# Reordering the turns of the local attention's software pipeline in an eight-core transformer kernel

## The reference

```python
q = l2norm(q) * qs;  k = l2norm(k) * ksc
q, k = rotary_xpos(q, k)
bq = q.reshape(b, h, w, 512, d) * 8.0
bk, bv = look_around(k windows), look_around(v windows)   # this window and the one before
sim = jnp.einsum('bhwid,bhwjd->bhwij', bq, bk)
mask = (i < j) | (i > j + 512) | (j == -1)
attn = softmax(where(mask, -max, sim), axis=-1)
out = jnp.einsum('bhwij,bhwjd->bhwid', attn, bv)
x = x + out @ wo
x = x + (a * gelu(g)) @ w2 + b2      # a, g = split(layernorm(shift(x)) @ w1)
```

## Time and profile before

| | us |
|---|---|
| median of the timed runs (2) | 6040.22 (6033.57 to 6046.87) |
| profiled execution, device time | 5998.51 |
| span of its slowest core (core 4) | 5996.8 |
| spans of the eight cores | 5910.4 to 5996.8 |
| PE, matmuls busy | 2880.4 (48%) |
| DVE busy | 2177.7 (36%) |
| ACT busy | 1038.4 (17%) |

### The profile page before, as it was taken

How to read it: one execution, slowest core, us unless ns; L and a number is a source line. 1 busy time by engine, 2 the same in 40 slices (tenths; PEclk the granted TensorE clock), 3 DMA queues, 4 the chain that set the end, 5 groups by cost and what they waited for, 6 DMA issues and landing times.

```text
span 5996.8 us, 43264 instructions; the slowest of 8 cores (5910.4 to 5996.8 us)
## 1 busy us (share of the span) xinstructions
PE 2880.4 (48%) x12576; PEld 1358.3 (23%) x12752; DVE 2177.7 (36%) x4629; ACT 1038.4 (17%) x1989; POOL 38.2 (1%) x46
## 2 busy tenths in 40 slices
PE   3322222232445454543776664454554545678632
PEld 2222222111212212221332221212221222233211
DVE  3666666642323323232233212323232332223324
ACT  0222222210211213031111101303121121011100
POOL 0000000000000000000000000000000000000000
PEclk9666666655556565655887776565555656698865
DMA  5000000014010010104500021010101008000022
GB/s 90 1 0 0 1 0 0 0 63 89 1 42 0 1 42 1 42 1 74 98 8 28 28 47 35 1 42 1 42 1 42 0 1 151 28 29 1 28 70 84
DMA packets 92663, 182.15 MB, mean 30 GB/s; under 512 B 2064, under 2 KB 20752, under 8 KB 92304
## 3 DMA queue, kind: packets, MB, share of 16 engines
q0 software_dynamic: 30176, 61.32, 6.4%
q1 hardware_dynamic: 62256, 118.07, 6.3%
HBM read 177.78 MB, written 54.53 MB: 39 GB/s over the span
## 4 chain that ended last, share of the span: by engine, by line
PE 44%; DVE 32%; issue 8%; DMA 7%; ACT 4%; another core or an unknown queue 3%; DVEq 2%; ACTq 0%; SPq 0%; POOL 0%; POOLq 0%
PE pb_l L1559 6%; PE pa_l L1034 5%; PE pa_l L1303 4%; PE pbf_l L1237 3%; PE bsa_l L1265 3%; DMA YBF<-ysp 3%; DVE RRF L1193 3%; PE pba_l L1509 3%; PE pbg_l L1523 3%; PE pb_l L1523 3%; PE pb_l L1509 3%; DMA ysp<-YBF 2%; PE pa_l L1149 2%; PE pa_l L1163 2%
## 5 line engine op out<-in xcount | busy, mean ns | idle before, releaser
L1237 PE MATMUL pbf_l<-CBF,PRB_l 128*128 128x128 bf16 x1280 | 177.4, 303 | 787.9 <-DVE PRB_l L1228 753.2
L1277 DVE CAST OH_l<-bsa_l 64x128 bf16<-64x128 f32 x256 | 72.4, 283 | 844.9 <-PE bsa_l L1265 844.9
L1559 PE MATMUL pb_l<-HACT_l,W2P_l 128*128 128x512 bf16 x1378 | 333.7, 405 | 44.8 <-DVE YBF L1575 29.4
L1205 ACT ACTIVATE PRB_l<-pa_l,RRF 128x512 bf16<-128x512 f32 x256 | 175.9, 687 | 979.6 <-DVE RRF L1201 975.9
L1237 PEld LDWEIGHTS pbf_l<-CBF,PRB_l 128*128 128x128 bf16 x1280 | 116.9, 131 | 840.1 <-issue 840.1
L634 PE MATMUL pb<-XKk,WR 128*128 128x256 bf16 x512 | 74.9, 321 | 384.1 <-DVE XKk L625 384.1
L1509 PE MATMUL pba_l<-HB_l,W1I_l 128*128 128x512 bf16 x690 | 183.8, 411 | 157.2 <-DVE HB_l L1486 115.9
L1303 PE MATMUL pa_l<-OH_l,WOF_l 64*128 64x512 bf16 x512 | 220.9, 628 | 32.3 <-DVE YBF L1317 27.4
L1009 PE MATMUL pa_l<-WQKV_l,HQ_l 128*128 128x512 bf16 x248 | 70.5, 453 | 311.7 <-DVE YLC L1000 160.7
L1250 ACT ACTIVATE PTB_l<-pbf_l 128x640 bf16<-128x640 bf16 x256 | 180.3, 704 | 206.8 <-PE pbf_l L1237 206.8
L1050 ACT ACTIVATE SQB_l<-pa_l 128x512 bf16<-128x512 f32 x64 | 38.2, 597 | 952.9 <-PE pa_l L1034 948.2
(11 more groups left out here) (223 smaller groups left out, 4460.1 us busy)
## 6 DMA issues: line engine op xcount, KB each, us to landing
YBF<-ysp SPq DMA_DIRECT2D x16, 2048.0 KB, 10.9
ysp<-YBF SPq DMA_DIRECT2D x16, 2048.0 KB, 7.2
W1I_l<-w1i POOLq DMA_DIRECT2D x10, 2048.0 KB, 54.7
W2P_l<-w2p POOLq DMA_DIRECT2D x10, 1024.0 KB, 91.2
ysp<-KF SPq DMA_DIRECT2D x8, 1024.0 KB, 4.4
RT_l<-rot SPq DMA_DIRECT2D x8, 1024.0 KB, 13.9
YF<-ysp SPq DMA_DIRECT2D x4, 2048.0 KB, 11.5
out<-OT SPq DMA_DIRECT2D x16, 512.0 KB, 2.6
```

What stands on the lines that cost most here:

```text
L1205: return e.activation(PRB[:, par, 0:512], sA[:, 0:512], AF.Exp, bias=nm, accum_out=s1c)
L1237: return e.transpose(PBF2[par][:, kk * 128:kk * 128 + 128], PRB[:, par, kk * 128:kk * 128 + 128], cbf("ident"))
L1559: return e.matmul(PB_[oc4][:], W2P[:, j, oc * 128:oc * 128 + 128], HACT[:, j, :], start=(j == 0), stop=(j == NJ - 1))
```

## The change

Only the body of the loop over the turns changes. The seven functions, the buffers and the 35 turns (`n_its + 3`) stay.

```diff
                 for it in range(n_its + 3):
                     if it < n_its:
                         sc_tok[it] = emit_scores(it)
-                    if 3 <= it <= n_its + 2:
-                        ptv_tok[it - 3] = emit_ptv(it - 3)
-                        emit_pv(it - 3, ptv_tok[it - 3])
                     if 1 <= it <= n_its:
                         emit_vmex(it - 1, sc_tok[it - 1])
+                        emit_vnorm(it - 1)
                     if 2 <= it <= n_its + 1:
-                        emit_vnorm(it - 2)
                         emit_tp(it - 2)
+                        ptv_tok[it - 2] = emit_ptv(it - 2)
+                    if 3 <= it <= n_its + 2:
+                        emit_pv(it - 3, ptv_tok[it - 3])
                 t_oh = p.tok("v")
```

## The result

The changed kernel takes 5581.72 us in the median (11 runs), the kernel before 5991.62 us (10 runs, where the two known ahead of the prediction had a median of 6040.22). The ratio is 0.931, 95% interval 0.927 to 0.935. The forecast was 5650 us, 390 us less than 6040, with a range of 5580 to 5715. The gain, 410 us by the medians, is near the forecast; the level is not: runs in which one die is held at a lower clock are left out of all ratios, and without the two such runs the changed kernel's median is 5574 us, under the lower end of the range.

The account below looks back on a forecast made before the run. A serial chain of DVE and PE, 6.07 us a turn, was taken to bound the loop. Turns of 4.49 us save 48.7 us a block, 390 us in 8 blocks: 6040.2 - 390 = 5650 us, range 5580 to 5715.

Parts of the forecast that it names:

- The ring of before: Loop before the change: a serial chain DVE, PE, DVE, closed by the output copy standing first on DVE; 6.07 us a turn.
- The ring after: Changed loop: maxima, exponentials on ACT, normalization, output copy, then the next maxima; 4.49 us a turn, with PE outside.
- the hand-over from ACT to DVE: Changed loop, from the end of the exponentials' row sum to the normalization's start: 0.24 us, at the low end 0.15.
- the wait: Changed loop, each turn: DVE's normalization waits for ACT's exponentials of its own tile, 1.72 us.
- the loop of before from which the gain was counted: One loop before the change, from first scores to output projection: 196.2 us, against 147.5 us after.
- ACT's place in the ring: Changed loop: the exponentials lie between maxima and normalization, so DVE waits for ACT 1.72 us a turn.
- PE's slack: Changed loop: PV ends early enough that its output copy could start 2.49 us before DVE reaches it.
- Outside the loop: Rest of the kernel, output projection included: no instruction moves, costed at nothing.
- The rising clock: Rival: the output projection behind the loop starts at 2.4 GHz, saving 116 us more, to 5534 us; chance 8%.
- The dearer wait for ACT: Rival: the row sum reaches DVE 0.4 us later in each of 256 turns, 102 us, to 5752 us; chance 6%.
- The ring through PE: Rival: DVE needs PV in its tile's own turn, 7.48 us a turn, 361 us slower, 6401 us; chance 3%.

Follow-up runs that it names:

- The control with more transposes: Kernel before with each tile's five transposes done three times over: 6230.29 us, ratio 1.039.
- both single moves: Kernel before with only the output copy moved last on DVE: ratio 0.875; kernel before with only the normalization one tile nearer: ratio 0.986.
- the two kernels that add work to each: Changed kernel with each tile's transposes done three times: 5594.47 us, ratio 0.937; changed kernel with the second exponential done twice: 5705.61 us, ratio 0.957.
- the 41 runs above: Unchanged kernel before, runs with granted clock on record: 18 below 5970 us have mean 0.646 to 0.650 on their slowest core, 19 above 6000 us 0.619 to 0.642.
- the narrow group: Unchanged kernel before: 12 of the 23 runs of two groups, at 5955 to 5967 us.

## Why the prediction was right, and where it was wrong

*The ring of before.* Right. The control with more transposes lengthens DVE's wait by just the PE time added, 1.07 us, and both single moves came out with the turns (3.06 and 5.79 us, forecast 3.07 and 5.75) that the ring and its slack give. The turn that was read, 6.07 us, doesn't stand for all: a few are longer, and the mean is 6.10.

*The ring after.* Right in its mechanism and nearly in size: forecast 4.49 us, measured 4.41 for most turns, 4.43 in the mean. The term that was mis-sized is the hand-over from ACT to DVE, taken as 0.24 and measured as 0.17, the value near the other bound (0.15). With it the wait is 1.65 us, forecast 1.72. A loop takes 146.0 us, forecast 147.5, which is 12 us in eight; the loop of before from which the gain was counted was 0.3 us shorter than the mean of the eight, which is 2 more. So the loops gave 404 us and not 390. ACT's place in the ring and PE's slack were shown by the two kernels that add work to each.

*Outside the loop.* Right: the projection takes 274.3 us before and after, and the medians differ by 6 us more than the loops, which is within the interval (0.927 to 0.935 is 48 us wide).

*The step that failed* is the last one of the sum, "The timed runs lie 41.7 us above it (median 6040.2), so I put the forecast at 6040.2 - 390 = 5650 us". It took the level of two timed runs for the kernel's own. Of the 68 us between 5650 and the measured 5582, 49 are that level (6040.2, where ten runs have 5991.6) and 20 the gain (410 for 390). The two runs, 6034 and 6047 us, lie above 37 of the 49 later runs of the same kernel, and the profiled execution carried the stretches at 0.81 on its slowest core. For the two timed runs no clock is on record: that they were high for the same reason is likely by the 41 runs above, but not shown. Less 404 us, the level of ten runs, 5991.6, gives 5588, and that of the narrow group, 5960, gives 5556; measured 5582 beside the first and 5563 beside the second.

A sign was in the trace of before: the granted clock by core, 0.643 and 0.644 on cores 4 and 5, 0.648 and 0.649 on the others but one. The spans by core, 5910 to 5997 us, tell less, since they differ by some 50 us in the fastest runs as well. I read the level as given and set the range, 5580 to 5715, about it; it should have reached down by the 45 us that those stretches were worth.

*The rivals.* The rising clock: it did not rise in the changed kernel's loop, and where it was made to rise the turn stayed the same and the projection ran at 0.50. The dearer wait for ACT: it was cheaper, 1.65 us for 1.72. The ring through PE: it stayed open by more than 1.07 us, the PE time that was added for nothing.

*What I didn't ask* is which part of the diff earns the gain. By the prediction's own terms the normalization's move puts the exponentials, 1.72 us with their hand-overs, into a ring which they had no part in, and the copy's move alone leaves 3.07 us. I had all the rows for it.

## What to carry to other kernels

In a software pipeline over in-order engines, first find the instruction that closes the ring; here it was a cheap copy that stood first on its engine and waited for the far end of the chain, and moving it alone was worth 745 us. The normalization moved nearer to its producer waits for it in every turn, 1.66 us here, so price each move of a diff by itself. And when a few runs are all there is, look at clock and span of each core before taking their time as the kernel's level.

## What the runs showed of the hardware that was not expected

- The output projection's 32 unbroken matmuls of 64 rows (13.8 us) run at a granted clock of 0.50 (1.2 GHz) in every kernel profiled here, also behind a loop whose mean was 0.68, though in that loop the clock was back at 0.50 for 13 us when the projection started.
- Ten more transposes of 128 rows a turn, and nothing else, raised the mean clock of the changed kernel's loop from 0.50 to 0.68 (0.60 to 0.71 over all loops and cores). The Trainium skill (TensorE: Matmul & The Clock Gate, Part 4) says that transposes don't bring the full clock; this trace doesn't agree. The same ten in the loop of the kernel before left it at 0.50 to 0.53.
- The granted clock of 0.81 in the 90 us shown of the feed-forward part came on two cores of a die (4 and 5 in one profile, with 0.81 and 0.79, and 6 and 7 in another, with 0.81 and 0.80), while the other two of the same die had 1.00 and 0.98. Elsewhere in these two profiles other cores have it too, and in the profile of the changed kernel none does. The Trainium skill (TensorE: Matmul & The Clock Gate, Part 1) tells of a peak-current limiter that takes the whole die to 13/16, which is 0.81; the level agrees, the reach doesn't.
- One hand-over, ACT to DVE, was 0.24 us behind a group of four squares and 0.17 us behind a row sum. Why they differ wasn't tried.
